# Latent attention: the causal mask added by VectorE in PSUM instead of by a bfloat16 product on TensorE

## What is computed

```
q = jnp.concatenate([q_nope, q_pe], axis=-1)
k = jnp.concatenate([k_nope, k_rope], axis=-1)
scale = 1.0 / np.sqrt(DN + DR).astype(np.float32)
scores = jnp.einsum('bqhd,bkhd->bhqk', q, k) * scale
mask = jnp.triu(jnp.full((seq_len, seq_len), -jnp.inf, jnp.float32), k=1)
probs = jax.nn.softmax(scores.astype(jnp.float32) + mask, axis=-1).astype(q.dtype)
out = jnp.einsum('bhqk,bkhd->bqhd', probs, v).reshape(bs, seq_len, H * DV)
```

## Time and profile before

| what | value |
|---|---|
| median of 3 runs | 2195.18 us (2195.17 to 2196.2) |
| the profiled execution's own time | 2192.79 us |
| its span in the trace | 2191.0 us |
| TensorE, VectorE, ScalarE busy, share of the span | 86%, 50%, 41% |
| latent attention, stage of the change | from about 1787 to 2113 us |

### The profile page before, as it was taken

One profiled execution on the slowest core, in us unless ns is written; L12 is line 12 of the kernel. 1 busy time (PEld: TensorE's weight loads), 2 busy tenths in 40 slices (PEclk: granted clock), 3 DMA queues, 4 the chain that ended last, 5 costly groups with the idle time before them and its releaser, 6 DMA issues. The chain is left out here.

```text
span 2191.0 us, 30217 instructions
## 1 busy us (share of the span) xinstructions
PE 1876.8 (86%) x10553; PEld 1279.1 (58%) x10553; DVE 1089.0 (50%) x1877; ACT 900.6 (41%) x1872; POOL 653.0 (30%) x513
## 2 busy tenths in 40 slices
PE   4499689999998498699999995399996679999997
PEld 3133367887886255588888873023335447777776
DVE  4476334444444354444444447387734425555533
ACT  1177433333332265333333331168861125555431
POOL 2000246656662100466566642100000132332300
PEclk9599889999999699699999997589997559999998
DMA  2700154444430700434444410930002200000000
GB/s 80 104 1 1 40 133 101 112 121 111 104 90 0 108 2 7 116 101 114 123 108 105 103 36 22 140 34 1 1 1 46 67 0 1 1 1 1 2 1 20
DMA packets 128442, 123.91 MB, mean 57 GB/s; under 512 B 81480, under 2 KB 108240, under 8 KB 128176
## 3 DMA queue, kind: packets, MB, share of 16 engines
q1 hardware_dynamic: 128336, 122.51, 24.9%
HBM read 113.83 MB, written 8.65 MB: 56 GB/s over the span
## 5 line engine op out<-in xcount | busy, mean ns | idle before, releaser
L667 DVE TENSOR_TENSOR e_inner_lo<-e_inner_b,e_inner_hi 128x512 fp32r<-128x512 f32 x192 | 251.4, 1309 | 391.7 <-ACT e_inner_hi L614 391.7
L647 POOL TENSOR_TENSOR e_wsilu<-e_silu_b,e_rw 128x512 f32<-128x512 f32 x192 | 261.9, 1364 | 211.8 <-ACT e_silu_b L621 158.6
L554 PE MATMUL psum<-e_x_hi,e_w_hi 128*128 128x512 f32 x768 | 305.4, 398 | 6.2 <-DVE e_inner_b L678 4.9
L554 PE MATMUL psum<-e_x_lo,e_w_hi 128*128 128x512 f32 x768 | 300.9, 392 | 0.0
L554 PE MATMUL psum<-e_x_hi,e_w_lo 128*128 128x512 f32 x768 | 300.4, 391 | 0.0
L621 ACT ACTIVATE e_silu_b<-psum 128x512 f32<-128x512 f32 x192 | 114.7, 597 | 364.5 <-PE psum L554 364.5
L655 POOL TENSOR_TENSOR e_w_lo<-e_w_raw,e_w_hi 128x384 fp32r<-128x384 f32 x180 | 215.4, 1197 | 134.2 <-ACT e_w_hi L608 112.8
L1202 DVE TENSOR_REDUCE c_mx<-psum 128x1 f32<-128x1024 f32 x128 | 151.3, 1219 | 62.8 <-PE psum L1079 62.8
L554 PEld LDWEIGHTS psum<-e_x_hi,e_w_hi 128*128 128x128 f32 x768 | 145.5, 189 | 48.6 <-DVE e_inner_b L678 18.7
L554 PEld LDWEIGHTS psum<-e_x_hi,e_w_lo 128*128 128x128 f32 x768 | 145.3, 189 | 31.1
L554 PEld LDWEIGHTS psum<-e_x_lo,e_w_hi 128*128 128x128 f32 x768 | 145.6, 190 | 29.5
(11 more groups left out here) (322 smaller groups left out, 3321.2 us busy)
## 6 DMA issues: line engine op xcount, KB each, us to landing
e_rw<-e_rw_dram SPq DMA_DIRECT2D x64, 384.0 KB, 5.8
e_rw<-e_rw_dram SPq DMA_DIRECT2D x64, 256.0 KB, 5.4
e_w_raw<-in_L_ffn_w_gate SPq DMA_DIRECT2D x64, 192.0 KB, 2.6
e_w_raw<-in_L_ffn_w_up SPq DMA_DIRECT2D x64, 192.0 KB, 2.6
e_w_raw<-in_L_ffn_w_down SPq DMA_DIRECT2D x32, 384.0 KB, 3.5
e_rw<-e_rw_dram SPq DMA_DIRECT2D x64, 128.0 KB, 5.3
a_qs<-a_parts_dram SPq DMA_DIRECT2D x12, 256.0 KB, 9.3
b_qs<-b_parts_dram SPq DMA_DIRECT2D x12, 256.0 KB, 9.2
```

The source lines that it names most:

```text
L554: last = nc.tensor.matmul(bank[u % 2][:], parts.up_or_gate(a, s, which, k, j), parts.x[b][:, k, h * HALF:(h + 1) * HALF], start=(n == 0), ...
L647: nc.gpsimd.tensor_tensor(wsilu[:, u % 2, :], silu[:, u % 2, :], rw[:, s, j, h * HALF:(h + 1) * HALF], ALU.mult).then_inc(weighted, 1)
L667: nc.vector.tensor_tensor(inner_parts[1][:, u % 3, :], inner[:, u % 2, :], inner_parts[0][:, u % 3, :], ALU.subtract).then_inc(low_made, 1)
```

## The change

The product that added the mask goes; the last product of the scores now ends the group of accumulation and signals `score_ready`. VectorE, before each maximum, adds the same 128 x 128 tile of 0 and -1e30 (bfloat16, in SBUF) to the diagonal tile of the scores in PSUM and writes it back there, then waits for its own add by a new semaphore, `masked`.

```diff
+    masked = core.sem(f"{tag}a_msk")
...
                 for x, y in PASSES:
                     for k0 in range(0, (t + 1) * P, HALF):
                         nk = max(min(HALF, (t + 1) * P - k0), WIDE)
-                        nc.tensor.matmul(out[:, k0:k0 + nk], q[x][:, i % 2, a, t * P:(t + 1) * P], kT[y][:, a, k0:k0 + nk],
-                                         start=(x, y) == PASSES[0], stop=False, skip_group_check=True)
-                nc.tensor.matmul(out[:, t * P:(t + 1) * P], core.ident_h[:], core.mask_h["prev"][:, 1, :],
-                                 start=False, stop=True, skip_group_check=True).then_inc(score_ready, 1)
+                        last = nc.tensor.matmul(out[:, k0:k0 + nk], q[x][:, i % 2, a, t * P:(t + 1) * P], kT[y][:, a, k0:k0 + nk],
+                                         start=(x, y) == PASSES[0], stop=(x, y) == PASSES[-1], skip_group_check=True)
+                last.then_inc(score_ready, 1)
...
             def maximum(i, t, a):
                 n = n_unit(i, t, a)
+                own = scores_of(a)[:, t * P:(t + 1) * P]
                 dve.wait_ge(score_ready, n + 1)
+                nc.vector.tensor_tensor(own, own, core.mask_h["prev"][:, 1, :], ALU.add).then_inc(masked, 1)
+                dve.wait_ge(masked, n + 1)
                 nc.vector.tensor_reduce(negmax[:, n % 4:n % 4 + 1], scores_of(a)[:, 0:(t + 1) * P], AX_X, ALU.max,
                                         negate=True).then_inc(negmax_ready, 1)
```

## The result

The changed kernel takes 2203.36 us against 2198.24 us for the kernel before (medians of 20 runs each, taken side by side): ratio 1.0024, 95% interval 1.0014 to 1.0033. It is slower by about 5.1 us. The forecast was 5.7 us.

A forecast was written before the change was run, and what follows sets the result against it. TensorE sets the pace nearly everywhere but waits at places for VectorE's copies behind the maximum. Six middle pairs (+3.7), first (+0.2) and last (+1.8) gave +5.7 us on 2195.2, so 2200.9 us, range 2195.0 to 2206.5.

The forecast's parts named there:

- d = 0.32 us: Before each maximum on VectorE: the add and the wait for it make the maximum end 0.32 us later.
- The rival at d = 0.29: Before each maximum: waiting for the add costs no extra 0.035 us; sum 3.8 us or less, 2195 to 2199, chance 0.35.
- the one at 0.45 to 0.5: Before each maximum: a dear add, from using or waiting on one PSUM bank; sum 14 us, 2209, chance 0.1.
- Step 0: +0.25: Step 0 of a middle pair: the copy TensorE waits for has no slack, so TensorE is 0.25 us later.
- Steps 1 and 2: 0.105 us saved each: Steps 1 and 2: projections cover VectorE's work and two mask products go, saving 0.105 us a step; TensorE's delay falls to +0.04.
- Rotation, GpSimd, inverse: +0.31: Step 4: the inverse's broadcast copy hangs on GpSimd, which hangs on the swap rotation, 0.31 us later; TensorE waits for it.
- GpSimd's start: Sign that the forecast is right: GpSimd starts 0.3 us later in a pair.
- my placing of VectorE's list: Steps 1 and 2: VectorE's instructions placed each behind its predecessor, putting the swap rotation 0.31 us later.
- the copy of step 3: Steps 3 and 4: the copy of group 0 makes values 0.14 us later than they would be, TensorE's delay +0.20.
- Steps 5 to 7: +0.08, +0.03, -0.01, then +0.21: Last steps of a middle pair: added delay less copy slack at the transposes, then group 1's values, taking TensorE to +0.62 us.
- Sum: Whole kernel: six middle pairs 3.7 us, first pair 0.2, last pair 1.8, together +5.7 us.
- The rival "TensorE's gain goes through": Where copies have 0.2 us slack TensorE does not wait for them, so the removal counts in full: -7.7 us, 2187.5, chance 0.05.

The follow-up runs named there:

- e9_add0: Kernel before, with VectorE's add in place of the mask product in step 0 only: middle pair 40.98 us against 40.72, ratio 1.0002.
- e2_nomask: Changed kernel with the add dropped too, so neither product nor add (mask left out, time only): middle pair 39.84 us, ratio 0.9955 to the kernel before.
- e10_add12: Kernel before, with the add in place of the product in steps 1 and 2 only: middle pair 40.60 us against 40.72, ratio 0.9997.
- e6_before_mixed: Kernel before, products kept, VectorE's copies moved ahead of maxima: group 0 in steps 0 and 4 to 7, group 1 in 0 and 7; pair 39.67 us, ratio 0.9975.
- e12_ahead: Kernel before, adds only in steps 4 to 6, copies ahead of maxima: group 0 in 0, 4 to 7, group 1 in 0, 5 to 7; pair 39.43 us, ratio 0.9962.
- e11_add37: Kernel before, with the add in place of the product in steps 3 to 7 only: middle pair 41.13 us against 40.72, ratio 1.0005.

## Why the prediction was right

The sign, the size (5.7 forecast, 5.4 in the stage, 5.1 in the medians) and the mechanism held. By its own steps:

- *d = 0.32 us.* Right. The add's record is 295 ns, the maximum starts 0.33 us after the add (1924.80 and 1925.13). The rival at d = 0.29 (no cost of the wait) and the one at 0.45 to 0.5 fall with it. The Trainium skill, "VectorE: DVE Perf Modes", section "The DRAIN you can't avoid", has no extra cost of the semaphore; the trace has 0.03 us between the add's end and the maximum, and an overlap of 0.07 us where nothing is waited for the earlier trace rows.
- *Step 0: +0.25.* Measured +0.27 at the start of score(1, 0); e9_add0 shows that it goes through the whole pair, +0.26.
- *Steps 1 and 2: 0.105 us saved each.* This is the term that was mis-sized. Starts of score(1, 0) and score(3, 0), before and after:

```profile
1918.53 0.39 PE L1610 MATMUL psum<-l_kT_hi,la_q_hi 128*128 128x256 f32 x1
...
1924.11 0.50 PE L1610 MATMUL psum<-l_kT_hi,la_q_hi 128*128 128x512 f32 x1
```

```profile
1931.34 0.39 PE L1611 MATMUL psum<-l_kT_hi,la_q_hi 128*128 128x256 f32 x1
...
1936.52 0.50 PE L1611 MATMUL psum<-l_kT_hi,la_q_hi 128*128 128x512 f32 x1
```

  With score(2, 0) between them (1920.94 and 1933.54) 0.21 and 0.19 us are saved, 0.10 a product. I had read the product's price off the start of what follows it, 0.04 us ahead of a projection, and missed that the projection's own first pass was 0.09 us longer behind it. Over a whole pair e2_nomask puts a product at 0.88 / 16 = 0.055 us. The Trainium skill, "TensorE: Matmul & The Clock Gate", section "Back-to-back issue gap", has 0.081 us; these runs have 0.10 in steps 1 and 2, and less in a pair because TensorE's waits for VectorE swallow part of it: in e2_nomask the wait of step 0 grows from 0.25 to 0.33 us and that of step 4 from 0.93 to 1.16.
- *Rotation, GpSimd, inverse: +0.31.* The chain was right, rotation and inverse moved by the same amount, but by 0.14 and 0.13 us; GpSimd's start, which I had named as a sign with 0.3 us, by 0.13. Of the missing 0.17 us about 0.09 are the larger saving in step 1: score(2, 0) starts 0.06 us later against the pair's start, where my steps had 0.15. The other 0.08 are in my placing of VectorE's list, which I took as back to back through both steps; in the trace its add of maximum(2, 0) starts at 1934.38, no later against the pair's start than the maximum did before, as it waits for score(2, 0). TensorE was thus 0.13 us ahead at score(3, 0), where I had it 0.04 behind, and the copy of step 3 then cost 0.15 (forecast 0.14). e10_add12 shows the link alone: rotation -0.11, inverse -0.12, pair -0.12.
- *Steps 5 to 7: +0.08, +0.03, -0.01, then +0.21.* From the inverse at +0.13 this pair went to +0.27 at score(6, 0), +0.38 at score(7, 0) and +0.55 at its end: +0.14, +0.11 and +0.17. Where TensorE now waits, what follows the wait is about 0.05 us longer as well: in step 5 the projection started 0.15 us after the transposes, now 0.20.
- *Sum.* Six middle pairs +3.16 us (forecast 3.7), last pair +1.56 (1.8). The first pair, from the first rotation to the inversion after it that begins the second pair, +0.68 (0.2). About 0.4 of this is not the change's: TensorE's clock rose to its upper level later in this execution, see below. So the nearness of 5.7 and 5.4 is in part luck: the steps' own sizes gave too much by 0.8 us in the middle and last pairs, errors of both signs cancelled within a middle pair (0.18 too much at the inverse, 0.11 too little behind it), and the first pair's clock made up for some of the rest.
- *The rival "TensorE's gain goes through"* had -7.7 us; e2_nomask has -6.65 us in the stage with no add at all, so the gain is real, and the add takes it back and 5.4 us more. The sum is -6.65 + 12.05.

## What to carry to other kernels

The sum of an engine's idle time does not tell what an instruction there will cost. Look for what is queued behind the place where it goes, and how long before its consumer's start that ended: here the same add cost 0.26 us in step 0, by a copy that stood behind the maximum, and nothing in steps 1 and 2, where the pair even became 0.12 us shorter. When work goes from the engine that sets the pace to a second one, reorder the second one's list as well: the order alone was worth 1.05 us of 40.7 in a pair (e6_before_mixed), twice what the change cost. A kernel with the change in some steps came out ahead only after a further reordering (e12_ahead, 0.24 us a pair under e6_before_mixed). And a step that is measured as "the next instruction starts 0.04 us later" is priced too low if the next instruction's own length changes with it.

## What the runs showed that I had not expected

A product of 128 columns ahead of a projection takes 0.04 us (bfloat16) or 0.06 us (fp32r) to the start of what follows, and lengthened the first pass behind it from 0.23 to 0.32 and 0.29 us.

TensorE's granted clock rose within the first pair, and not at the same place of the program in each execution. Windows of before, then of the changed kernel (columns as in the earlier trace rows; the clock is the third number from the end):

```profile
1791.00:1794.00 3.00, 0.16 (x2) 0.03 (x1) 0.42 (x1) 0.46 (x1) 2.37 (x2) 1.00 0.00 0
1795.00:1800.00 5.00, 5.00 (x18) 3.39 (x18) 1.58 (x3) 1.60 (x7) 0.00 (x0) 0.50 0.02 3
```

```profile
1801.00:1806.00 5.00, 0.97 (x6) 0.67 (x4) 1.47 (x5) 1.32 (x3) 3.39 (x3) 0.50 0.00 0
1807.00:1812.00 5.00, 5.00 (x19) 3.81 (x17) 2.57 (x6) 0.99 (x4) 0.00 (x0) 0.50 0.00 0
1813.00:1818.00 5.00, 4.77 (x40) 3.64 (x35) 2.73 (x7) 1.96 (x5) 4.46 (x4) 1.00 0.00 0
```

In the execution of before the clock is at its upper level (1.00) from about 1790.7 to 1794.3, most of it while TensorE waits for ScalarE, falls back to the lower level (0.50) and rises for good at about 1800.8, 29.1 us after the first rotation. All twelve experiments have such a first stretch; only this execution of the changed kernel has none, and its clock rises at about 1812.7, 29.9 us after the rotation. The first stretch gave nothing, as the next projection starts 23.05 and 23.06 us after the rotation in the two. The later rise did: from the projection of step 2 to score(3, 0) it is 1.77 us before and 2.13 here, where a middle pair takes 1.46 and 1.39, so about 0.4 us.

The broadcast copy of the inverse (VectorE, SBUF to SBUF) takes 0.43 us with GpSimd idle and 1.02 to 1.17 with GpSimd at work; in both traces it ended 0.28 us after GpSimd's instruction, whenever it had started. This is what ties TensorE to the rotation. It makes a delay ahead of the inverse in steps 3 and 4 free (e11_add37: 0.16 us later at score(4, 0), 0.01 at the inverse), and one ahead of the rotation go through to the inverse (e9_add0: 0.27 us at both).
